# Cross-attention encoder layer on one core: the last group's low parts, scale and sums on other engines and by batch, and two stacks' q transfers and a q rounding at other places of the prologue

## What is computed

```python
q = (query @ Wq + bq).reshape(b, s, 16, 16).transpose(0, 2, 1, 3)
k = (key @ Wk + bk)...;  v = (values @ Wv + bv)...
scores = jnp.einsum('bhqd,bhkd->bhqk', q, k) / jnp.sqrt(16.)
scores = jnp.where(j < i, scores, -1e30)
attn = softmax(scores); attn = attn.at[:, :, 0, :].set(0.0)
attn_out = (attn @ v) @ Wo + bo
x = layer_norm(query + attn_out, ln1_g, ln1_b)
ffn = jax.nn.relu(x @ W1 + b1) @ W2 + b2
out = layer_norm(x + ffn, ln2_g, ln2_b)
```

## Time and profile before

| | |
|---|---|
| median of 3 runs | 1667.87 us (1667.69 to 1668.47) |
| the profiled execution | 1669.3 us |
| its span, first to last instruction | 1667.4 us |
| TensorE matmul busy | 1619.5 us, 97% of the span |
| weight load | 1592.4 us, 95% |
| ScalarE / VectorE / GpSimd busy | 1549.0 / 1432.2 / 1386.5 us |
| mean granted TensorE clock | 0.983 of full speed |
| chain that ended last, TensorE's share | 94% |

### The profile page before, as it was taken

The page is one execution under the profiler, slowest core; times in us unless marked ns, Lnnn a source line. Parts: engine busy times, 40 slices in busy tenths (PEclk is TensorE's granted clock), DMA queues, the critical chain, the costliest instruction groups (busy, mean ns, idle before and its releaser), DMA issues.

```text
span 1667.4 us, 54091 instructions
## 1 busy us (share of the span) xinstructions
PE 1619.5 (97%) x16700; PEld 1592.4 (95%) x16700; DVE 1432.2 (86%) x6735; ACT 1549.0 (93%) x5907; POOL 1386.5 (83%) x1358
## 2 busy tenths in 40 slices
PE   4799999999999999999999999999999999999997
PEld 3699999999999999999999999999999999999996
DVE  3688898898898898898898898898898889889874
ACT  3799999999999999999999999999999999999993
POOL 2368888888888888888888888888888888888896
PEclk7799999999999999999999999999999999999999
DMA  7856656656666655665665665665665665665520
GB/s 146 174 118 123 131 134 121 131 126 127 133 135 116 135 133 117 136 134 120 132 137 117 132 134 121 135 131 126 127 134 126 128 130 128 127 130 130 112 60 27
DMA packets 307071, 208.99 MB, mean 125 GB/s; under 512 B 164320, under 2 KB 281952, under 8 KB 306784
## 3 DMA queue, kind: packets, MB, share of 16 engines
q1 hardware_dynamic: 305088, 204.60, 59.6%
q10 hardware_dynamic: 1696, 0.92, 0.3%
HBM read 104.73 MB, written 50.33 MB: 93 GB/s over the span
## 4 chain that ended last, share of the span: by engine, by line
PE 94%; DMA 1%; SPq 1%; DVE 1%; ACT 1%; issue 1%; POOL 1%; POOLq 0%; ACTq 0%; DVEq 0%
PE ps_dense L377 32%; PE ps_dense L387 32%; PE ps_probsT L480 14%; PE ps_scores L470 7%; PE ps_att L498 7%; PE ps_dense L359 2%; ACT probs L575 0%; DMA k_spill<-kT 0%; SPq L278 0%; DMA k_stack<-k_spill 0%; POOL hT L1014 0%; DMA probs<-in_L_xattn_Wk_dram 0%; SPq L235 0%; DMA q_stack<-qT 0%; SPq L241 0%
## 5 line engine op out<-in xcount | busy, mean ns | idle before, releaser
L575 ACT ACTIVATE probs<-ps_scores,negmax 128x128 f32<-128x128 f32 x2048 | 744.2, 413 | 8.4 <-DVE negmax L782 5.0
L1006 POOL TENSOR_TENSOR probs<-probs,recip 128x512 f32<-128x512 f32 x512 | 534.2, 1044 | 136.7 <-DVE recip L765 136.5
L782 DVE CUSTOM_DVE_ANT_0 ps_scores<-ps_scores,mask 128x128 f32<-128x128 f32 x2048 | 527.6, 319 | 71.8 <-PE ps_scores L470 69.6
L575 ACT ACTIVATION_READ_ACCUMULATOR probs<-ps_scores,negmax 128x1 f32 x2048 | 517.4, 253 | 0.0
L387 PE MATMUL ps_dense<-w,hT 128*128 128x256 f32 x3072 | 420.9, 286 | 1.8 <-DVE u L903 0.9
L377 PE MATMUL ps_dense<-zT,w 128*128 128x256 f32 x3072 | 416.9, 285 | 0.5 <-DVE h_f L866 0.5
L1014 POOL TENSOR_TENSOR hT<-h_f,hT 128x512 fp32r<-128x512 f32 x256 | 327.6, 1294 | 93.3 <-DVE h_f L866 93.3
L377 PEld LDWEIGHTS ps_dense<-zT,w 128*128 128x128 f32 x3072 | 381.8, 189 | 0.9 <-issue 0.9
L387 PEld LDWEIGHTS ps_dense<-w,hT 128*128 128x128 f32 x3072 | 380.3, 188 | 2.3 <-issue 1.2
L592 ACT ACTIVATE probsT<-ps_probsT 128x508 f32<-128x508 f32 x512 | 319.2, 623 | 40.3 <-PE ps_probsT L480 40.1
L480 PE MATMUL ps_probsT<-ident,probs 128*128 128x128 f32 x2048 | 314.9, 276 | 0.0
(11 more groups left out here) (84 smaller groups left out, 2335.3 us busy)
## 6 DMA issues: line engine op xcount, KB each, us to landing
k_stack<-k_spill SPq DMA_DIRECT2D x384, 128.0 KB, 4.4
q_stack<-qT SPq DMA_DIRECT2D x762, 64.0 KB, 2.0
k_spill<-kT SPq DMA_DIRECT2D x128, 256.0 KB, 2.2
c_tok<-in_ctx_dram SPq DMA_DIRECT2D x256, 64.0 KB, 4.8
x_res<-in_x_dram SPq DMA_DIRECT2D x64, 256.0 KB, 3.1
out_dram<-o_tok SPq DMA_DIRECT2D x64, 256.0 KB, 2.8
x_tok<-in_x_dram SPq DMA_DIRECT2D x252, 64.0 KB, 2.4
probsT<-in_L_xattn_W_dram SPq DMA_DIRECT2D x1, 1024.0 KB, 11.1
```

The costliest lines, as they stand in the source:

```text
L575: last = nc.scalar.activation(probs[:, m % 4, i, :], ps_scores[m % 2][:, i, :], ACT.Exp, bias=negmax[:, m % 4, i:i + 1], scale=-1.0, accum ...
L782: last = nc.vector.tensor_tensor_reduce(ps_scores[m % 2][:, i, :], ps_scores[m % 2][:, i, :], mask[:], -1.0, -MASKED, ALU.add, ALU.min, ac ...
L1006: nc.gpsimd.tensor_tensor(probs[:, m % 4], probs[:, m % 4], recip[:, m % 4, :].unsqueeze(2).broadcast_to([P, 4, S]), ALU.mult)\
```

## The change

For the last group only: `h_lo` moves from GpSimd to VectorE, directly after each `h_full`. The second batch of the down projection gathers in a free score bank (`last_half`), and TensorE signals the first batch by itself; `last_sum` adds and takes statistics batch by batch. Scale and offset of the output move from GpSimd to VectorE (`last_out`), by batch, and the store is split in two. In the prologue: the second half of the q stacking of group 0 goes from SyncE's list to GpSimd's, ahead of two memsets; `q_hi(1)` and `x_hi(2)` go behind the exponentials of unit (0, 1), `x_flips(2)` behind the maxima of unit (0, 1), `q_lo(1)` behind those of unit (0, 2).

```diff
--- before.py
+++ after.py
@@ -161,6 +161,7 @@
         s_hhi = [sem(f"h{n}_hi") for n in range(4)]
         s_kzero = sem("k_stacks_zeroed")
 
+        s_qfirst = sem("first_q_stacked_by_pool")
         s_qstack = [sem(f"q_stacked{i}") for i in range(2)]
         s_kspill = [sem(f"k_{half}_in_dram") for half in ("hi", "lo")]
         s_kstack = sem("k_stacked")
@@ -191,10 +192,15 @@
         s_og = sem("z2_scaled")
         s_o = sem("o_ready")
         s_out = sem("out_stored")
+        s_first_half = sem("last_f2_first_batch_full")
+        s_last = sem("last_scaled")
+        s_sum0 = sem("last_sum_first_batch")
 
         def f32(ap):
 
             return ap.bitcast(F32)
+
+        last_half = ps_scores[0][:, 0:2].rearrange("p h k -> p (h k)")
 
         WEIGHTS = [(Wq, wq, KC, D), (Wk, wk, KC, D), (Wv, wv, KC, D), (Wo, wo, KC, D), (W1, w1, KC, FF),
                    (W2, w2, FC, D)]
@@ -286,7 +292,11 @@
                     sp.dma_start(x_res[:], x_v[g]).then_inc(s_xres, 16)
 
             def store(g):
-                if exists(g):
+                if g == NG - 1:
+                    for b in range(GB):
+                        sp.wait_ge(s_o, NG + b)
+                        sp.dma_start(out_v[g][:, b], o_tok[:, b]).then_inc(s_out, 16)
+                elif exists(g):
                     sp.wait_ge(s_o, g + 1)
                     sp.dma_start(out_v[g], o_tok[:]).then_inc(s_out, 16)
 
@@ -323,7 +333,6 @@
             stack_k(0, 0, True)
             stack_k(0, 1, True)
             load_x(2)
-            stack_q(0, 1, True)
             load_c(2)
             load_weight(2)
             load_weight(3)
@@ -332,7 +341,7 @@
             load_weight(4)
             for it in ITERATIONS:
                 iteration(it)
-            sp.wait_ge(s_out, 16 * NG)
+            sp.wait_ge(s_out, 16 * (NG + 1))
 
 
         @block.tensor
@@ -379,12 +388,13 @@
                                                 start=(n == 0), stop=(n == len(steps) - 1))
                 last.then_inc(full[name], 1)
 
-            def tokens_product(name, w, acts, b, kcs, total, starts=True):
-
+            def tokens_product(name, w, acts, b, kcs, total, starts=True, home=None):
+
+                home = ps_dense[BANK[name]][:, b * D:(b + 1) * D] if home is None else home
 
                 for kc in kcs:
                     for n, (a, c) in enumerate(SPLIT):
-                        last = nc.tensor.matmul(ps_dense[BANK[name]][:, b * D:(b + 1) * D],
+                        last = nc.tensor.matmul(home,
                                                 acts[:, a, kc, b * S:(b + 1) * S], w[:, c, kc, :],
                                                 start=(starts and kc == 0 and n == 0),
                                                 stop=(kc == total - 1 and n == len(SPLIT) - 1),
@@ -452,7 +462,10 @@
                         pe.wait_ge(s_hlo[2 * half], g + 1)
                         pe.wait_ge(s_hlo[2 * half + 1], g + 1)
                     last = tokens_product("f2", w2, hT, b, range(4 * half, 4 * half + 4), FC,
-                                          starts=(b == 0))
+                                          starts=(b == 0 or g == NG - 1),
+                                          home=last_half if g == NG - 1 and b == 1 else None)
+                    if q == 2 and g == NG - 1:
+                        last.then_inc(s_first_half, 1)
                     if q == 3:
                         last.then_inc(full["f2"], 1)
 
@@ -461,7 +474,9 @@
                     return
                 b, w = m // 4, m % 4
                 if m < 2:
-                    pe.wait_ge(s_qstack[m], 16 * 2 * PARTS * (g + 1))
+                    if g == 0 and m == 1:
+                        pe.wait_ge(s_qfirst, 16 * 2 * PARTS)
+                    need(pe, s_qstack[m], 16 * 2 * PARTS * (g + 1 - m))
                     pe.wait_ge(s_kstack, 16 * 2 * PARTS * (g + 1))
                 need(pe, s_exp, g * UNITS + m - 1)
                 bank = ps_scores[m % 2]
@@ -576,6 +591,9 @@
                                                 bias=negmax[:, m % 4, i:i + 1], scale=-1.0,
                                                 accum_out=sums[:, m % 4, i:i + 1])
                 last.then_inc(s_exp, 1)
+                if g == 0 and m == 1:
+                    q_hi(1, True)
+                    x_hi(2, True)
 
             def take_probsT(g, m):
                 if not exists(g):
@@ -604,7 +622,7 @@
                                      ACT.Copy).then_inc(s_done, 1)
 
             def x_hi(g, first=False):
-                if exists(g) and (g > 0 or first):
+                if exists(g) and (g not in (0, 2) or first):
                     round_hi(xT, x_flip, g, s_xflip, s_hi["xT"], full["q"], g)
 
             def c_hi(g, first=False):
@@ -639,9 +657,11 @@
                     act.dma_start(RAW[0][0][0][32 * j:32 * j + 32], rows[j]).then_inc(s_w[0], 16)
 
             def q_hi(g, first=False):
-                if exists(g) and (g > 0 or first):
+                if exists(g) and (g > 1 or first):
                     for i in range(2):
-                        need(act, s_qstack[i], 16 * 2 * PARTS * g)
+                        need(act, s_qstack[i], 16 * 2 * PARTS * (g - i))
+                    if g == 1:
+                        act.wait_ge(s_qfirst, 16 * 2 * PARTS)
                     projection_hi(g, "q", qT, bq_col)
 
             def k_hi(g, first=False):
@@ -783,6 +803,10 @@
                             ps_scores[m % 2][:, i, :], ps_scores[m % 2][:, i, :], mask[:], -1.0, -MASKED, ALU.add,
                             ALU.min, accum_out=negmax[:, m % 4, i:i + 1])
                     last.then_inc(s_max, 1)
+                    if g == 0 and m == 1:
+                        x_flips(2, True)
+                    if g == 0 and m == 2:
+                        q_lo(1, True)
 
             def take_lo(name, dst, g):
 
@@ -867,6 +891,10 @@
                             h_f32[:, n % 2, i, :], ps_dense[BANK[f"f1_{n}"]][:, i * GT:(i + 1) * GT],
                             b1_col[:, 2 * n + i:2 * n + i + 1], 0.0, ALU.add, ALU.max)
                     last.then_inc(taken[f"f1_{n}"], 1)
+                    if g == NG - 1:
+                        dve.wait_ge(taken[f"f1_{n}"], g + 1)
+                        nc.vector.tensor_tensor(hT[:, 1, 2 * n:2 * n + 2, :], h_f32[:, n % 2],
+                                                f32(hT[:, 0, 2 * n:2 * n + 2, :]), ALU.subtract).then_inc(s_hlo[n], 1)
 
             def att_lo(g):
                 if exists(g):
@@ -912,8 +940,30 @@
                 if exists(g):
                     moments(0, g, s_st1, s_mv1, s_ve1, s_of1)
 
+            def last_sum():
+                g = NG - 1
+                dve.wait_ge(s_yb, g + 1)
+                need(dve, s_og, g)
+                for b, (s_full, count) in enumerate(((s_first_half, 1), (full["f2"], g + 1))):
+                    dve.wait_ge(s_full, count)
+                    nc.vector.tensor_tensor(u2[:, b, :], last_half if b else ps_dense[BANK["f2"]][:, 0:D], y_b2[:, b, :],
+                                            ALU.add).then_inc(s_sum0, 1)
+                    dve.wait_ge(s_sum0, b + 1)
+                    nc.vector.bn_stats(stats[:, 1, b, :], u2[:, b, :]).then_inc(s_st2, 1)
+
+            def last_out():
+                g = NG - 1
+                need(dve, s_out, 16 * g)
+                for b in range(GB):
+                    dve.wait_ge(s_z2, GB * g + b + 1)
+                    nc.vector.tensor_tensor(o_tok[:, b, :], u2[:, b, :], g2_row[:], ALU.mult).then_inc(s_last, 1)
+                    dve.wait_ge(s_last, b + 1)
+                    nc.vector.tensor_tensor(o_tok[:, b, :], o_tok[:, b, :], be2_row[:], ALU.add).then_inc(s_o, 1)
+
             def norm2_sum(g):
-                if exists(g):
+                if g == NG - 1:
+                    last_sum()
+                elif exists(g):
                     dve.wait_ge(full["f2"], g + 1)
                     dve.wait_ge(s_yb, g + 1)
                     need(dve, s_og, g)
@@ -922,7 +972,7 @@
                       .then_inc(taken["f2"], 1)
 
             def norm2_stats(g):
-                if exists(g):
+                if exists(g) and g < NG - 1:
                     statistics(1, u2, g, taken["f2"], s_st2)
 
             def norm2_moments(g):
@@ -978,6 +1028,7 @@
             q_lo(0, True)
             for it in ITERATIONS:
                 iteration(it)
+            last_out()
 
 
         @block.gpsimd
@@ -993,6 +1044,9 @@
                                     pattern=[[-1, P]], channel_multiplier=1).then_inc(s_const, 1)
             nc.gpsimd.memset(f32(k_stack[0][:]), 0.0).then_inc(s_kzero, 1)
             pool.wait_ge(taken["q"], KC)
+            for s, half in enumerate(QPART):
+                for j in (2, 3):
+                    nc.gpsimd.dma_start(f32(q_stack[0][32 * s:32 * s + 32, j]), f32(qT[32 * j:32 * j + 32, half])).then_inc(s_qfirst, 16)
```

## The result

The changed kernel ran in 1665.84 us (median of 22 runs), the kernel before beside it in 1668.68. The ratio is 0.9981, 95% interval 0.9976 to 0.9987: 3.2 us faster, 0.19%. Applied to the 1667.87 us that stood ahead of the prediction it is 1664.7. Forecast were 1663.3 and a range of 1659.8 to 1666.5, so 4.6 us were forecast and about 3.2 came. By my own bound of 0.2% this lies a hair inside "same". The profiled spans are 1667.4 before and 1663.8 after, 3.6 us apart, and in these two traces all of the difference lies in the last 18 us: the prologue brought nothing that shows, the tail nearly twice what I gave it.

What follows compares the result with a forecast made beforehand. From about 90 us the kernel was taken as one TensorE matmul stream, so only edits ahead or behind count. Prologue 2.5 plus tail 2.05 gave 4.6 us off the median 1667.87: 1663.3, range 1659.8 to 1666.5.

Steps and rivals of the forecast that it cites:

- Prologue, 2.5 us forecast: Start of the kernel: earlier scores and k(1) spill bring unit (1, 0) forward by 2.5 us, from 0 to 4.7.
- T0: Prologue: start of scores unit (0, 0), forecast at 28.9 because group 0's k lands 1.7 us later.
- GpSimd's six issues: Prologue: q transfers issued by GpSimd from 16.00, taken at 1.0 us each, bounds 0.64 and 1.7.
- the gate of unit (1, 0): Prologue: unit (1, 0) waits for group 1's k, whose spill gains 2.5 us or nothing; 2.5 carried past it.
- rival (b): Prologue's gain ends at the k gate, unit (1, 0) within 0.5 us of 57.49; 1665.5, chance 0.20.
- Its sign: Prologue, sign of a wrong forecast: unit (1, 0) at the same distance from its k issues but at 57.
- I had weighed it for 0.8 us: Prologue: if several issuing engines save only sequencer time, k's delay is 2.5 us and the part brings 0.8 less.
- Tail, 2.05 us forecast: After the stream: low parts, sum and statistics, scale and offset save 0.15 + 0.55 + 1.35 us, from 1.5 to 3.3.
- end of the last matmul: Tail, down projection of group 63: second half starts at 1654.7 instead of 1654.86 with GpSimd first, 0.15 us won.
- rival (a): Tail: VectorE's last low-part subtraction takes the port ahead of GpSimd's scale; 1.05 us more, 1662.2, chance 0.24.
- one of my signs of being wrong: Tail: the first batch's sum waiting for `y_b2` would show the forecast wrong; no size given.
- rival (c): Prologue: GpSimd's issues so slow that the q half lands late, at 40 for 3.2 us each; 1671.5, chance 0.06.

Runs made afterwards that it cites:

- e3_q_on_sync: The full change with the second half of group 0's q issued by SyncE again instead of GpSimd; span 1663.9 in one profiled execution.
- e7_late_subtraction: The full change with three small reciprocals on VectorE ahead of the last low-part subtraction; first h_hi to the end 19.07 us, 1.2 more than the change.
- the tail alone: The kernel before with only the last group's edits, prologue unchanged; ratio 0.9976 (0.9967 to 0.9985) to the kernel before, span 1662.5.
- e4_rows_late: The full change with six bias rows (768 KB) loaded behind group 1's k stack instead of ahead; ratio 0.9967 to the kernel before, span 1660.8.
- e10_kept_busy: The full change with 28 useless transposes filling TensorE's wait ahead of unit (1, 0); ratio 0.9996 to the kernel before, profiled span 1664.0.

## Why the prediction was right and where it was wrong

**Direction and size.** Faster was right, by 3.2 us instead of 4.6. Two terms missed in opposite directions: the tail's surplus of 1.5 us stood in for more than half of the prologue's missing 2.5. That the total came so near is in good part luck.

**Prologue, 2.5 us forecast, nothing that shows measured.** Nearly every step up to the last held:
- T0, k(0)'s landing behind the moved q transfers: forecast 28.9, measured 28.71 (a delay of 1.5 for the 1.7).
- GpSimd's six issues: 3.16 us, 0.53 each, for the 1.0 taken and below my lower end of 0.64:

```profile
15.98 3.16 POOL L1049 DMA_DIRECT2D q_stack<-qT  x6 [10.62 <-DVE qT L852]
```

- unit (0, 2): 32.4 and 32.21; end of the small matmuls: 53.6 and 52.94.
- The step that failed is the gate of unit (1, 0): "k(1)'s spill gains 2.5 or nothing", of which I took the 2.5 and carried it to the end. The spill's issue did gain 2.2 us, but I took its time to land as a constant. It was 5.2 us instead of 3.1, with the q transfer just ahead of it slowed alike (4.7 for 3.3), and with 768 KB taken out of the queue that q transfer landed in 2.0 and the spill in 2.4 and 4.6; 2.7 us of SyncE's 3.75 were gone already at `load_c(2)`, whose four issues took 4.82 us where they had taken 2.10, and ended at 27.26. SyncE's issue slots were not the resource that was short. DMA time was, and the moved transfers only changed the engine that issues them. That the traffic was at its limit stood in the earlier trace rows, share 1.18 from 20 to 30 us, and I used it for k(0) but not for k(1). This is rival (b): I gave it 0.20, with the tail at its lower value. Its sign came too, unit (1, 0) at the same distance from its k issues and at 57.56; "near 55" and an earlier stream did not.

What the Trainium skill says in DMA: Bandwidth & Descriptors, Issuing engines are not separate DMA queues, is borne out by `e3_q_on_sync` and the spill: another issuing engine saved issue time, and no DMA time. I had weighed it for 0.8 us; it was worth the whole term.

**Tail, 2.05 us forecast, 3.6 measured in the span.**

| term | forecast | measured |
|---|---|---|
| end of the last matmul | 0.15 (rival (a): 1.2) | 1657.95 to 1656.76: 1.2 |
| sum, statistics, moments to ScalarE's start | 0.55 | 3.16 to 2.57: 0.6 |
| norm, scale, offset | 1.35 | 3.77 to 2.37: 1.4 |
| last output to the end of the span | 0 | 2.52 to 2.10: 0.4 |

The first is the order that I called wrong. The two starts, 1652.84 and 1652.85 by my sum, were 1652.84 and 1652.87 in the trace. The instant was right, and "each small delay on VectorE's longer chain decides for it" was not: nothing delayed VectorE, in this trace or in the seven others. I had treated as a coin what falls the same way each time. `e7_late_subtraction` shows that the price on either side was right too, 1.2 us measured for 1.05. The last term stood in the sum at nothing: the second store moves 128 KB instead of 256 and lands in 1.7 us, the one for group 62, and the last of the kernel before, in 2.1.

The split of the sum by batch brought less than it can: batch 0's half was ready at 1655.3, but its sum waited for `y_b2` until 1655.96. It cost next to nothing, since batch 1 was ready at 1656.76 and its sum started 0.04 later. That wait was one of my signs of being wrong, and it was a poor one.

**Chances.** The outcome is (a) and (b) together, which I had as alternatives. They are independent: one is in the tail, one in the prologue. Written as a product, with both at one half, the centre would have been about 1664 (an estimate: half of 1.05 off and half of 2.2 onto 1663.3), and same would have had more than 0.28. In rival (c) the last figure doesn't follow from its own rule: a half that lands at 40 gives about 1675, not 1671.5. Nothing else rests on it.

**Still open.** What makes the stretch between unit (1, 0) and the stream 1.3 us longer in some executions than in others. Full clock at unit (1, 0) alone doesn't explain it. Whether the tail alone (0.9976) is faster than the full change (0.9981) isn't decided by their intervals.

## What to carry to other kernels

A transfer moved to another engine's queue frees issue slots and not DMA time: before a gain is carried through a later transfer, read the DMA share of the stretch where that one will run, and where it is near 1 let the landing time grow by what the issue gains. A gain ahead of a gate is worth nothing until the gate moves, and then it is (2 us here). Where two engines reach a shared port within a few hundredths of a microsecond, price both orders as two outcomes, and look for the cheap edit that fixes the order. Before a difference of 1 us between two traces is put down to an edit, look at what two executions of the same code differ by.

## What the runs showed of the hardware

A DMA issued by GpSimd took 0.53 us of its list (3.16 / 6), less than one of ScalarE's (3.81 / 6 = 0.64). A VectorE subtraction of two SBUF operands that came 0.20 us after a GpSimd operation ended 0.55 us behind it; where it came 0.03 us ahead, GpSimd's took 1.81 us instead of 1.29. The last 64 KB q transfer ahead of k(1)'s spill landed in 4.7 us in the changed kernel, in 3.3 in the kernel before and in 2.0 in `e4_rows_late`. In `e10_kept_busy` the granted clock fell to 0.52 between 54 and 56 us while TensorE was fed without a gap:

```profile
54.00:56.00 2.00, 2.00 (x13) 2.00 (x11) 0.00 (x0) 0.17 (x1) 0.18 (x1) 0.52 1.14 121
```

What it was fed with were the 32 small matmuls from 49.66 and the transposes from 53.16; up to 54 the granted clock had been 1.00.
